# Linear attention, FFN and two layer norms on one core: the activations of the out and FFN projections split to fp16 in rows and turned by DMA

## The reference

```python
qkv = x @ Wqkv + bqkv                      # split in q, k, v; 16 heads of 32
q_prime = exp(q @ omega - 0.5 * |q|^2)     # omega: 32 x 128; the same for k
k_sum = sum over the sequence of k_prime
k_v = k_prime^T v                          # 128 x 32 for each head
out = (q_prime @ k_v) / (q_prime . k_sum + 1e-06)
x = layernorm(x + out @ Wout + bout)
pooled = x.reshape(..., 8, 64).sum(axis=-2)
x = layernorm(x + x @ weight^T + pooled @ disha)
```

## Time and profile before

| | |
|---|---|
| three runs | 2627.39, 2633.75, 2639.04 us; median 2633.75 |
| profiled execution | span 2625.4 us from first to last instruction; the page gives no other time of its own for it |
| PE (TensorE matmul) busy | 2449.6 us, 93% of the span |
| DVE (VectorE) busy | 2012.5 us, 77% |
| ACT (ScalarE) busy | 1114.5 us, 42% |
| POOL (GpSimd) busy | 513.1 us, 20% |
| DMA | 214.96 MB moved, mean 82 GB/s |
| mean granted TensorE clock | 0.982 of 2.4 GHz |

### The profile page before, as it was taken

One profiled execution on the slowest core, in us unless ns is written; L12 is line 12 of the kernel. 1 busy time (PEld: TensorE's weight loads), 2 busy tenths in 40 slices (PEclk: granted clock), 3 DMA queues, 4 the chain that ended last, 5 costly groups with the idle time before them and its releaser, 6 DMA issues.

```text
span 2625.4 us, 64569 instructions
## 1 busy us (share of the span) xinstructions
PE 2449.6 (93%) x24576; PEld 1402.6 (53%) x24576; DVE 2012.5 (77%) x3966; ACT 1114.5 (42%) x1921; POOL 513.1 (20%) x522
## 2 busy tenths in 40 slices
...
PEclk9898999999999999999999999999999999999998
...
DMA packets 85263, 214.96 MB, mean 82 GB/s; under 512 B 19312, under 2 KB 21456, under 8 KB 80720
## 3 DMA queue, kind: packets, MB, share of 16 engines
...
...
## 4 chain that ended last, share of the span: by engine, by line
PE 85%; DVE 8%; issue 3%; ACT 2%; SPq 1%; DMA 1%; POOL 0%; DVEq 0%; POOLq 0%; ACTq 0%
PE bank_y L365 23%; PE bank_a L365 23%; PE bank_x L365 12%; PE bank_kf L405 4%; PE bank_qf L449 4%; PE bank_x L478 4%; PE kv_ps L423 2%; PE kv_ps L428 2%; PE bank_nm L465 2%; PE bank_nm L467 2%; PE bank_nm L466 2%; PE kv_ps L426 2%; DVE k_feat_lo L660 2%; PE bank_x L375 1%; PE bank_a L375 1%
## 5 line engine op out<-in xcount | busy, mean ns | idle before, releaser
L777 POOL TENSOR_TENSOR rstd<-mean_var,minus_half 128x1 f32<-128x1 f32 x256 | 166.8, 652 | 1770.8 <-DVE mean_var L615 1770.8
L534 ACT ACTIVATE k_feat<-bank_kf 128x512 f32<-128x512 f32 x512 | 305.7, 597 | 253.0 <-PE bank_kf L405 239.6
L660 DVE TENSOR_TENSOR k_feat_lo<-k_feat 128x512 bf16<-128x512 f32 x512 | 362.6, 713 | 60.6 <-ACT k_feat L534 54.7
L667 DVE TENSOR_TENSOR q_feat_lo<-q_feat 128x512 bf16<-128x512 f32 x512 | 355.4, 704 | 29.9 <-ACT q_feat L543 26.7
L543 ACT ACTIVATE q_feat<-bank_qf 128x512 f32<-128x512 f32 x512 | 305.5, 597 | 164.9 <-PE bank_qf L449 138.7
L549 ACT ACTIVATE at_hi<-bank_x 128x512 f16<-128x512 f32 x128 | 76.4, 597 | 396.6 <-PE bank_x L478 396.6
L365 PE MATMUL bank_a<-xt_hi,wqkv_hi 128*128 128x512 f16 x480 | 187.6, 391 | 46.4 <-POOL xt_lo L759 26.0
L423 PE MATMUL kv_ps<-v_hi,k_feat 128*128 128x33 f16 x2048 | 208.3, 179 | 11.4 <-DVE k_feat_lo L660 9.9
L405 PE MATMUL bank_kf<-omega_s,stack_k 98*128 98x128 f16 x2048 | 200.6, 220 | 17.4 <-ACT k_feat L534 14.9
L449 PE MATMUL bank_qf<-stack_q,omega_s 98*128 98x256 f16 x1024 | 197.0, 274 | 15.4 <-ACT q_feat L543 15.2
L365 PE MATMUL bank_y<-wffn_hi,yt_hi 128*128 128x512 f16 x512 | 195.7, 382 | 16.3 <-DVE yt_lo L715 14.5
...
## 6 DMA issues: line engine op xcount, KB each, us to landing
xt_f<-xt SPq DMA_DIRECT2D x33, 1024.0 KB, 5.0
stack_k<-t_hi_k SPq DMA_DIRECT2D x256, 128.0 KB
stack_q<-t_hi_q SPq DMA_DIRECT2D x256, 128.0 KB
rows<-x SPq DMA_DIRECT2D x128, 256.0 KB, 2.8
out<-rows SPq DMA_DIRECT2D x128, 256.0 KB, 2.0
stack_k<-t_lo_k SPq DMA_DIRECT2D x128, 128.0 KB
stack_q<-t_lo_q SPq DMA_DIRECT2D x128, 128.0 KB
stack_k<-half_norm SPq DMA_DIRECT2D x256, 4.0 KB
```

The source lines that it names most:

```text
L534: nc.scalar.activation(k_feat[:, i % 2, :], bank_kf[:, :], ACT.Exp, scale=1.0 / WS).then_inc(S["k_exp"], 1)
L660: v.tensor_tensor(k_feat_lo[:, u, :], k_feat[:, u, :], k_feat_hi[:, u, :], ALU.subtract).then_inc(S["kfl"], 1)
L667: v.tensor_tensor(q_feat_lo[:, at, :], q_feat[:, at, :], q_feat_hi[:, at, :], ALU.subtract).then_inc(S["qfl"], 1)
```

## The change

- `ident` and the pieces AT and YT on TensorE go: 256 groups of four fp32 transposes, and with them their turns in `bank_x`.
- ScalarE (AT, YT) now writes the fp16 hi half in rows, `at_row[:, 0]` or `y_row[:, 0]`, from `attn` or `rows` in SBUF; VectorE writes the lo half beside it. Both have one buffer, so ScalarE waits before each until the transpose of the tile before has landed (`at_moved`, `y_moved`).
- SP turns both halves by one DMA transpose for each tile (`turn`): 128 x 1024 fp16 (256 KB) into `at_t` or `yt_t`, 8 blocks of 128 x 128, two buffers. These are TA i and TY i in SP's list, 256 in all. WO and FF wait for their landing.
- `squares` becomes one tensor for k and q. For that KN moves ahead of QP0, KP3 and QP0 change places, and QN moves ahead of KP0. `kv_f` gets its own memory, and some of the places in which weights are staged at the start move.
- VectorE's AT is no longer one place later than in TensorE's list.

```diff
 ORDER = """
-KP0. KF7' KP0 QN' KF8' KV6' Z0' FF1'. KV7' FF1' AT2' KF9' KV8' KP1. NM6' KP1 KF10' NM7' WO2'. KV9'
-WO2' AT3' QF0 KF11' KP2. Y2' KV10' Z1' KP2 QP0. KF12' KV11' QF1 QP0 WO3'. KV12' QF2 KF13' WO3' YT2'
-KP3. KF14' QF3 KP3 KV13' QF4 KF15' QP1. KV14' Y3' QF5 KN QF6 QP1 FF2'. QF7 KV15' FF2' KFIN' VP0.
+QN' KP0. KF7' KP0 KF8' KV6' Z0' FF1'. KV7' FF1' AT2' KF9' KV8' KP1. NM6' KP1 KF10' NM7' WO2'. KV9'
+WO2' AT3' QF0 KF11' KP2. Y2' KV10' Z1' KP2 KP3. KF12' KV11' QF1 KP3 WO3'. KV12' QF2 KF13' WO3' YT2'
+KN QP0. KF14' QF3 QP0 KV13' QF4 KF15' QP1. KV14' Y3' QF5 QF6 QP1 FF2'. QF7 KV15' FF2' KFIN' VP0.
 YT3' Z2' VP0 NM0 FF3'. FF3' NM1 VP1. AT0 NM2 VP1 QF8 Z3' KF0 NM3 QP2. QP2 KF1 WO0. KV0 QF9 WO0 KF2
 VP2. AT1 KV1 QF10 Y0 VP2 KF3 QF11 WO1. QF12 YT0 KV2 QF13 WO1 QF14 QP3. KF4 QF15 XS QP3 KV3 Y1 VP3.
 VP3 KV4 FF0. KF5 NM4 FF0 YT1 KV5 KF6 NM5
 """
...
-DVE_LAGS = {"AT": 1, "FF": 1, "KF": 1, "KP": 1, "QF": 1, "QN": 2, "QP": 1, "VP": 1, "WO": 2, "YT": 2, "Z": 1}
+DVE_LAGS = {"FF": 1, "KF": 1, "KP": 1, "QF": 1, "QN": 2, "QP": 1, "VP": 1, "WO": 2, "YT": 2, "Z": 1}
...
-XT NRQ' ST0' ST1' STK LX1 LX0 NRK ST2' ST3' LX3 LX2 STQ
+XT NRQ' ST0' TA2' TA3' ST1' TY2' STK LX1 LX0 NRK TY3' ST2' TA0 ST3' LX3 LX2 TA1 TY0 STQ TY1
...
-        at_hi, at_lo = (sb(f"at_{s}", [P, KB, P], F16) for s in ("hi", "lo"))
-        yt_hi, yt_lo = (sb(f"yt_{s}", [P, 2, KB, P], F16) for s in ("hi", "lo"))
+        at_row, y_row = (sb(n, [P, 2, D], F16) for n in ("at_row", "y_row"))
+        at_t, yt_t = (sb(n, [P, 2, 2 * KB, P], F16) for n in ("at_t", "yt_t"))
...
+            def turn(source, made, freed, target, moved, n, i):
+
+                wait(sp, made, n)
+                carry()
+                wait(sp, freed, n - 2)
+                carry()
+                sp.dma_start_transpose(target[:, i % 2, :, :], source[:, :, :].rearrange("p s n -> p (s n)")
+                                       ).then_inc(moved[i % 2], 16)
...
+                if kind == "TA":
+                    turn(at_row, "at_lo_done", "wo_done", at_t, at_moved, TPC * j + i + 1, i)
+                elif kind == "TY":
+                    turn(y_row, "y_lo_done", "ff_done", yt_t, y_moved, TPC * j + i + 1, i)
...
-                elif kind in ("AT", "YT"):
-                    if kind == "AT":
-                        wait(pe, "normed", 8 * j + 2 * i + 2)
-                    else:
-                        wait(pe, "y_done", TPC * j + i + 1)
-                    bank_free(b, c, kind, i)
-                    src = attn[:, :] if kind == "AT" else rows[:, i, :]
-                    for kb in range(KB):
-                        last = nc.tensor.transpose(bank_x[:, P * kb:P * (kb + 1)],
-                                                   src[:, P * kb:P * (kb + 1)], ident[:, :])
-                    last.then_inc(S["at_done" if kind == "AT" else "yt_done"], 1)
                 elif kind in ("WO", "FF"):
                     if what == "first":
-                        wait(pe, "at_lo_done" if kind == "WO" else "yt_lo_done", TPC * j + i + 1)
+                        wait(pe, (at_moved if kind == "WO" else y_moved)[i % 2], 16 * (2 * j + i // 2 + 1))
...
                 elif kind == "AT":
-                    wait(act, "at_done", TPC * j + i + 1)
-                    wait(act, "wo_done", TPC * j + i)
-                    nc.scalar.activation(at_hi[:, :, :], bank_x[:, :].rearrange("p (k n) -> p k n", k=KB),
-                                         ACT.Copy).then_inc(S["at_hi_done"], 1)
+                    wait(act, "normed", 8 * j + 2 * i + 2)
+                    wait(act, at_moved[(i - 1) % 2], 16 * (2 * j + (i - 1) // 2 + 1))
+                    nc.scalar.activation(at_row[:, 0, :], attn[:, :], ACT.Copy).then_inc(S["at_hi_done"], 1)
...
                 elif kind == "AT":
                     wait(dve, "at_hi_done", n)
-                    v.tensor_tensor(at_lo[:, :, :], bank_x[:, :].rearrange("p (k n) -> p k n", k=KB),
-                                    at_hi[:, :, :], ALU.subtract).then_inc(S["at_lo_done"], 1)
+                    v.tensor_tensor(at_row[:, 1, :], attn[:, :], at_row[:, 0, :],
+                                    ALU.subtract).then_inc(S["at_lo_done"], 1)
```

More of the change, by code:

```diff
@@ L69 @@
 KP0. KF7' KP0 KV6' KF8' KP1. KFIN' KV7' KF9' KP1 KV8' KF10' KV9' KP2. KF11' KP2 KF12' KV10' KP3.
-KV11' KF13' KP3 KV12' KF14' KV13' KF15' KV14' QP0. QP0 KN VP0. QP1. QP1 VP0 QP2. KV15' QP2 VP1. VP1
+KV11' KF13' KP3 KV12' KF14' KV13' KF15' KV14' KN QP0. QP0 VP0. QP1. QP1 VP0 QP2. KV15' QP2 VP1. VP1
 VP2. QP3. XS QP3 VP2 KF0 KF1 VP3. KV0 KF2 VP3 KV1 KV2 KF3 KF4 KV3 KF5 KF6 KV4 KV5
@@ L369, in _, with halves @@
             w3, xt_p = {"hi": wqkv_hi, "lo": wqkv_lo}, {"hi": xt_hi, "lo": xt_lo}
-            at_p, wo_p = {"hi": at_hi, "lo": at_lo}, {"hi": wout_hi, "lo": wout_lo}
-            yt_p, wf_p = [{"hi": yt_hi[:, u, :, :], "lo": yt_lo[:, u, :, :]} for u in range(2)], {"hi": wffn_hi, "lo": wffn_lo}
+            wo_p, wf_p = {"hi": wout_hi, "lo": wout_lo}, {"hi": wffn_hi, "lo": wffn_lo}
+            def halves(turned, i):
+                return {"hi": turned[:, i % 2, 0:KB, :], "lo": turned[:, i % 2, KB:2 * KB, :]}
             def norms(done):
@@ L376, in norms @@
                                             bank_a[32 * g:32 * (g + 1), :],
-                                            norm_w[:, :], squares[done[0]][:, g, :], start=True, stop=True,
+                                            norm_w[:, :], squares[:, g, :], start=True, stop=True,
                                             skip_group_check=True)
@@ L521, in step @@
                     if i == 0:
-                        wait(act, "qn_done", jq)
+                        wait(act, "kn_done", min(kA + 1, B * CPB) if isinstance(b, int) else kA + 1)
                     square("q", bank_x, i, 0)
@@ L672, in step @@
                     wait(dve, "nm_done", 8 * (j + 1))
-                    wait(dve, "kn_done", kA + 2 if runs(b, c + 1, "KN") else kA + 1)
                     for uu in range(2):
```

52 lines of the change are left out of this document (21 added, 31 removed).

## The result

| | before | after |
|---|---|---|
| median of the runs | 2633.94 us | 3263.7 us |
| range | 2627.39 to 2639.04 | 3260.44 to 3265.65 |
| profiled execution, span | 2625.4 us | 3263.5 us |
| mean granted TensorE clock | 0.982 | 0.91 |

The change makes the kernel slower: the ratio is 1.239, with an interval of 1.2371 to 1.2409. The sign was forecast, with a chance of 0.94; the size was missed. The forecast was 2991 us, and 3263.7 lies 14 us above the upper end of the range.

What follows compares the result with a forecast made beforehand. TensorE's list was taken to bound the steady part. Per slot -3.5 - 0.3 + 9.1 + 2.6 + 2.0 + 2.0 = +11.9 us, over 27 slots +321, with the drain +357: forecast 2991 us, range 2850 to 3250.

Steps and rivals of the forecast that it cites:

- the removal: Transposes taken off TensorE: -3.5 us a steady slot, and -0.3 us for waits that hang on bank_x.
- FF3', FF1', WO1 and the clock: Per steady slot, TensorE waits 9.1 us at FF3', 2.6 at FF1', 2.0 at WO1; lower clock adds 2.0.
- VectorE's y_lo is not what is late: At FF3', TY3' is held by SP's issue order, not y_lo; before the change yt_lo was there at FF3'.
- L: Time of one DMA transpose from issue to landing: 3.5 us, with ends of 2.0 and 5.0.
- The clock: TensorE falls to its lower level, 1.2 GHz, after long waits: 2.0 us a slot, between 0 and 3.5.
- The drain: Outside the steady part, 18 TensorE waits grow by about 3 us each, less 18 us: +36 us, ends 15 and 65.
- the 40 groups outside: Transpose groups outside the 27 full slots; taking them off TensorE is worth up to -18 us.
- both engines have slack, so I cost them at nothing: ScalarE's and VectorE's hi and lo copies stay as many, only their source becomes SBUF: no cost in the steady part.
- The hidden landing: Rival: TY3' lands within TensorE's 9.7 us after KF15', so only the removal is left: 2513 us, chance 0.04.
- Slow transposes, block after block: Rival: eight blocks turned one after another, L about 10 us, near 4000 us; chance 0.10 together with the in-between case.
- The time of 3250 to 3600 us: In-between case: L of 5 to 7 us, or transposes holding SP's issue long; chance 0.10 together with slow transposes.
- What would show it: Signs: no ident row, 27 or more bank_y waits, TensorE near 78%, steady slot 87 us, lower clock after long waits.

Runs made afterwards that it cites:

- 9: Old piece order, nothing turned, and VectorE writes at_lo as attn minus attn without waiting for ScalarE: 2585.47 us, 0.9807 of the kernel before.
- 6: Changed kernel with nothing turned, but the old piece order, separate squares for k and q and one at_row buffer: 2649.44 us, 1.0049 of the kernel before.
- 5: Changed kernel and its piece order, but SP issues no transposes and WO and FF read the unturned rows: 2804.53 us, 1.0633 of the kernel before.
- 11: Changed kernel's order with all DMA transposes issued by SP, but the products read the unturned rows: 2798.62 us, 1.0622 of the kernel before.
- the second run: Changed kernel with TY3' issued right behind the stack copies of k, ahead of the loads and half norm copies: 3139.62 us, 1.1924 of the kernel before.
- the mixed version: Kernel before with only y-row tiles 0 and 2 turned by DMA: 2646.41 us; with the last four chunks all over TensorE: 2624.8 us.

## Why the prediction was wrong

All runs in the three parts of the span, by the marks of SP (us against before; a slot is the 26 slots' mean):

| | per slot | 26 slots | behind the last mark |
|---|---|---|---|
| 9: nothing turned, old order, no stall | -0.6 | -16 | -20 |
| 6: the same with VectorE's stall | +1.6 | +41 | -20 |
| 5: and the new order, shared `squares` | +6.9 | +180 | -13 |
| 11: and all transposes, unread | +6.9 | +179 | -17 |
| after: and TensorE waits for them | +20.1 | +522 | +103 |
| predicted | +11.9 | | +36 |

Read down the column, each line adds one thing: 2.2 us a slot for the stall, 5.4 for the order, nothing for issue and traffic, 13.2 for the landings with their clock. Beside the forecast's 11.9 us a slot that is 5.4 more because the removal brought nothing, 5.4 more for the order, and 2.5 less for the landings: 20.2. The range was missed by the first two and by the drain.

- **FF3', FF1', WO1 and the clock**, 9.1 + 2.6 + 2.0 + 2.0 = 15.7 us a slot predicted, 13.2 measured. This mechanism was right in the main, and sized a little too high. In the slot above the three waits are 7.80, 3.06 and 1.68 us. At FF3' two errors went against each other: TY3' landed 19.9 us after KF15', not 18.8 (SP started the stack copies 1.8 us behind it, for 0.5; TY2' costs 1.23 us, not the 0.37 of a plain issue), and TensorE needed 13.1 us for its own way there, not 9.7, since QP1 (2.07 us) and QF6 (0.69 us) now waited too. That SP's order is the cause is true in part: "VectorE's y_lo is not what is late" was read from before, where nothing had to land behind it. As the second run shows, SP's order adds 1.9 to 5.3 us to the time at which y_lo is there, and with TY3' issued at once FF3' still waited up to 4.7 us.
- **L**: 3.5 predicted, 3.1 measured. The Trainium skill (Advanced Engine Details and Errata, X-Bar Transpose (TRN2)) has such transposes as fast as regular DMAs, which gave 2.8. Here the plain copy of the same bytes landed after 2.3 us and the transposes after 3.1; most of the way, but not equal. SP's issue is over twice as long, which is nearly the whole difference.
- **The clock**: 2.0 us a slot were taken, within 0 to 3.5. The price is 122 us over the whole span. Behind the last mark TensorE is busy 262 us, and 232 in the eleventh run, so 30 of the 122 lie in the drain and at most 3.5 us in each of the 26 slots: the high end of what was taken. The step counted only the work behind FF3'; from 1359.15 to 1362.47 in the trace of after, behind a wait of 2.15 us at KP3, the steps are 0.42 us as well.
- **The drain** failed by size: +36 predicted, +103 measured, and of that the landings with their clock are 121 (from -17 to +103). From 2900 us on 25 waits for landings sum up to 111.7 us, 4.5 us each, where I had grown 18 waits by 3 us. Where no k or v work is left, landings show that the steady part had hidden, and the clock is 0.78. The other half of that term was right: the 40 groups outside were to bring 18 us, and the drain of the ninth and sixth is 20 us shorter.
- **The step that failed by mechanism is "both engines have slack, so I cost them at nothing".** The removal was to bring 3.8 us a slot and cost 1.6. A mean of 80% says nothing of a stretch in which VectorE works without a gap. There its stall at AT went straight to TensorE (`k_feat_lo`), 64 us in all, and the ninth run shows it. Even without the stall only 0.6 of the 3.8 us arrived. TensorE's waits from 300 to 2300 us are then 84 us against 33, some 2 us a slot. The rest I couldn't place: over the span TensorE's busy time fell by 81 us (2449.6 to 2368.8), though 113 us of work were taken off. I also wrote that only the source of the copies moves to SBUF. That does something of its own. In the sixth run, over the whole span, the mean of y_row's subtraction was 791 ns for yt_lo's 683 (at_row's 696 for at_lo's 686), and GpSimd's rstd took 929 ns for 652. The Trainium skill has a rule for this (SBUF — State Buffer, SBUF: two separate sides): a VectorE operation with two inputs in SBUF and a GpSimd operation that reads SBUF exclude each other at a shared pair of ports. The traces agree, as the last section shows, but no run separates what this is worth in time.
- **The step that isn't there at all is the order of the pieces.** The diff's new `ORDER` was read only for where FF3', WO1 and FF1' stand. It cost 5.4 us a slot, 155 us between the sixth and the fifth run, nearly half of the forecast's whole loss. KP2 and KP3 became neighbours in `bank_a`, QP0 and QP1 in `bank_x`, QF5 and QF6 in `bank_qf`. For each pair the second piece waits for VectorE's or ScalarE's last read of the first. The trace of before had the rows to price it, for a piece in `bank_a`, its last matmul and its lo half:

```profile
1348.18 0.38 PE L365 MATMUL bank_a<-xt_lo,wqkv_hi 128*128 128x512 f16 x1
...
1349.89 0.75 DVE L623 SCALAR_TENSOR_TENSOR t_lo_k<-bank_a,bias_qk,t_hi_k 128x512 f16<-128x512 f32 x1 [1.19 <-ACT squares_k L507]
```

The bank is read until 1350.64, 2.2 us after the next piece could have begun; the waits in after are up to 2.6 us.

- **The rivals.** The hidden landing was wrong at FF3' by far, as argued; for tiles 0 and 2 of the y rows in the steady part it holds, which is what the mixed version lives on. Slow transposes, block after block, did not happen: eight blocks land in 3.1 us. The time of 3250 to 3600 us came without the mechanism that I gave for it.
- **What would show it**: no row with `ident`, 27 waits and more at `bank_y`, TensorE at 77% for 78%, and the lower level of the clock behind FF3' are there. The slot of 87 us is 97. Two small slips in the working change nothing: KF2's exp is 0.60 us long in the earlier trace rows, not 0.55, and the low end of the drain comes to 10 us by its own terms, not 15.
